# A recurrence step whose reset gate is formed ahead of the reciprocal, and inner norms scaled on VectorE

## The chip, the core and the metric

One core of a Trainium2 chip runs the whole program. The metric is the device time of one execution in microseconds (us). Engines are named as in the profile: PE is the matrix engine (PEld its weight loads), DVE the vector engine, ACT the scalar engine, POOL the GpSimd engine, SP the engine that issues most DMAs.

## What is computed

The input x is 4 batches of 512 tokens of width 128. Four layers follow one another, each added to x: a transformer block with self and context attention, a causal attention block with a dense mixture of 8 experts, a recurrent decoder, and an expert-choice mixture. The change is in the third layer and in the part of the second that runs beside it.

The recurrent layer takes 512 steps, one for each token, and each needs the state of the one before:

```
proj = h @ W
attn = softmax(enc_hiddens . proj)            # 77 context rows
context = attn @ enc_hiddens
gx = concat([x_t, context]) @ kernel + bias   # columns for z, r, candidate
gh = h @ recurrent_kernel
z = sigmoid(xz + hz);  r = sigmoid(xr + hr)
cand = tanh(xh + r * hh)
h = z * h + (1 - z) * cand
```

The layer in front of it, whose tail is computed beside the recurrence, has these norms; g and b are the norm's gain and bias, `layernorm` subtracts the mean and multiplies with the root of 1/(variance + eps):

```
h = layernorm(out, g, b)        # norm "g" of the names below, ahead of the experts
...experts weighted by a gate...
y = layernorm(moe, g, b)        # norm "h": added to x
x = layernorm(x + y)            # norm "i": the recurrence's input; norm "j" stands before the last layer
```

## The kernel before

Function `recurrence` runs both. Its "main" work is a Python loop over t in 0 to 511 that is unrolled on every engine. The order on each engine's queue is written out by hand; engines wait for one another through semaphores, and an instruction that waits holds back everything behind it on its engine.

The main chain of a step, by the lines of the profile: PE forms the scores from the state (L2068, L2074) and the state's own gate products (L2080). DVE takes the maximum of the scores (L2583) and copies the own products (L2589 or L2591, tile `own`). ACT makes the exponentials `p_t` (L2248), not yet divided by their sum. PE multiplies them with a table `gate_w` (helper `gate_products`, L1818): first the 32 columns for r together with two columns that give the sum of the exponentials (`ps_r`, `ps_total`, 34 columns), then the 64 columns for candidate and z (`ps_cz`). DVE takes the reciprocal of the sum (L2593, `rtotal`), then `pre_r` = r's product * rtotal + own (L2596), and `own` <- the other products * rtotal + own (L2599). ACT takes tanh of half of pre_r (L2251) and of half of pre_z (L2253). DVE forms the candidate's argument with a scan (L2603, `c_in`), ACT its tanh (L2255), DVE transposes (L2608, L2610) and forms the next state with another scan (L2614), on which PE's L2068 of the next step waits.

Beside this, each step carries pieces of "background" work, for the token tiles g = 1, 2, 3 (tile 0 is done before): attention in units (8 head pairs times 4 batches, a unit starting every 2 steps for g = 1 and 2, every 3 steps for g = 3), then the norm g and the gates, then 32 chunks of expert work, then the norms h and i, which give the recurrence the input of its next 128 steps. Three tables name the steps: attention of g starts at step 0, 110 and 219; the norm g at 71, 181 and 325; experts at 76, 186 and 330; the norms h and i (table `FIRST`) at 113 and 120, 223 and 231, 367 and 373. So the norms h and i of tile g fall into the attention of tile g + 1, and those of tile 3 into steps with little other work. Norm j stands at 383, 392 and 401. On PE background stands in `after_gates` (behind the gate products, ahead of the next L2068) and `ahead_of_gates` (ahead of the gate products). On ACT it stands in `after_exp` (ahead of L2251) and `after_candidate` (behind the step's last main operation), on DVE in `before_maximum` and `after_maximum`, both ahead of `own`. POOL runs `after_history`, at its own pace.

A norm takes these steps counted from its FIRST: 0 statistics (DVE, L2370), 1 moments (DVE, L2375), 2 `norm_scales` on POOL (L2271 to L2277: add eps, power -0.5, mean * rstd, times -1; 4 instructions), 3 `normalise` on ACT (L2111: two tiles in `after_exp`, two in `after_candidate`), 4 `turn_rows` on PE (L1931) and `take_rows` on ACT. For h there is no turn: POOL multiplies with the gain at step 4 (`gain_rows`, L2284) and adds to x at step 5 (`add_rows`, L2289). `BULK` names the steps behind norm i in which PE forms the input products for the next 128 tokens (L1985), one batch a step, four steps.

POOL also scales attention probabilities (`scale_probs`: a power, L2300, and a multiplication, L2304, which waits for the step's `c_in`) and forms the power for the query and key norms (L2296). PE turns the scaled probabilities (L1894).

## Time and profile before

| | us |
|---|---|
| median of 3 runs | 2823.57 |
| lowest and highest | 2823.46, 2825.21 |
| the profiled execution | 2822.87 |
| its span in the trace | 2821.0 |
| busy in the span: PE, DVE, ACT, POOL | 2447.3, 1887.3, 1567.0, 1002.9 |

The recurrence begins at 908 us (first L2583) and its last state is ready at 2707 us, so it takes 1799 us of the span, 3.51 us a step. A row of the timeline gives start, duration, engine, line, operation, what it writes and reads, and how often; in brackets stands the idle time of the engine before it and what ended it. The duration holds the time until the result is written; the next instruction of the same engine that waits for nothing may start before that.

### The profile page before, as it was taken

To read this page: it belongs to the slowest core of one execution; us is meant where nothing else is said; L and a number is where in the kernel's file an instruction comes from. 1 tells how busy PE (TensorE), PEld (TensorE's weight loads), DVE (VectorE), ACT (ScalarE), POOL (GpSimd) and SP (SyncE) were. 2 spreads that over 40 slices of the span, in tenths; PEclk is the share of its full clock that TensorE was granted. 3 is DMA by queue.
4 is the path that set the end of the run, shared out by engine and by line. 5 is a ranking of instruction groups with operands and counts; after the bars stand their busy time and mean duration, and the time that the engine had idled before them with its cause. 6 is when DMAs were issued, how large, how long until landed. Compare 5 with 4: busy or idle time off the path is not lost. (4 is left out here: it accounts for less than half of the span.)

```text
span 2821.0 us, 137474 instructions
## 1 busy us (share of the span) xinstructions
PE 2447.3 (87%) x57364; PEld 1663.9 (59%) x57364; DVE 1887.3 (67%) x7210; ACT 1567.0 (56%) x5258; POOL 1002.9 (36%) x2005
## 2 busy tenths in 40 slices
PE   6999999988988999798999897998879777666669
PEld 4666666666555555565555565666656545444449
DVE  4666666775553777677677677777767766776553
ACT  4777777643453666576666575666657443333322
POOL 2000000042110676466677465566636311001026
PEclk9999999999999999999999999999999999999989
DMA  4000000000012000011100010100001000000013
GB/s 155 5 5 5 5 8 5 2 12 5 14 37 72 24 19 15 11 43 31 27 17 15 14 44 23 27 11 14 8 7 43 6 20 7 6 7 7 6 49 88
DMA packets 51898, 64.80 MB, mean 23 GB/s; under 512 B 7432, under 2 KB 36560, under 8 KB 51152
## 3 DMA queue, kind: packets, MB, share of 16 engines
q1 hardware_dynamic: 47184, 50.32, 5.9%
q8 instruction: 456, 7.47, 1.1%
q0 software_dynamic: 4096, 5.67, 1.0%
q14 instruction: 162, 1.33, 0.2%
HBM read 46.38 MB, written 9.60 MB: 20 GB/s over the span
## 5 line engine op out<-in xcount | busy, mean ns | idle before, releaser
L2330 POOL TENSOR_TENSOR gru_terms<-gru_states,gru_signs 128x8 f32<-128x8 f32 x512 | 104.3, 204 | 687.6 <-DVE gru_states L2614 687.1
L2068 PE MATMUL gru_ps_sr<-score_w,gru_states 128*32 128x78 f32 x4096 | 175.1, 243 | 183.3 <-DVE gru_states L2614 173.7
L2248 ACT ACTIVATE gru_p_t<-gru_ps_tc,gru_negmax 128x12 f32<-128x12 f32 x512 | 138.9, 271 | 338.6 <-DVE gru_negmax L2583 322.0
L2251 ACT ACTIVATE gru_th_r<-gru_pre_r 128x32 f32<-128x32 f32 x512 | 119.2, 233 | 303.5 <-DVE gru_pre_r L2596 303.4
L2304 POOL TENSOR_SCALAR bg_probs<-bg_probs,bg_arsum 128x256 f32<-128x256 f32 (+2 forms) x192 | 240.9, 1255 | 86.4 <-DVE gru_c_in L2603 80.4
L1818 PE MATMUL gru_ps_tc<-ctx_gate_w,gru_p_t 128*4 128x64 f32 x12288 | 267.8, 219 | 2.0 <-issue 1.9
L1818 PE MATMUL gru_ps_sr<-ctx_gate_w,gru_p_t 128*4 128x34 f32 x12288 | 189.4, 194 | 78.7 <-ACT gru_p_t L2248 76.3
L2068 PEld LDWEIGHTS gru_ps_sr<-score_w,gru_states 128*32 128x32 f32 x4096 | 81.0, 107 | 292.2 <-DVE gru_states L2614 273.9
L313 ACT ACTIVATE self_probs<-self_sc,self_negmax 128x512 f32<-128x512 f32 x256 | 176.7, 698 | 112.1 <-DVE self_negmax L351 112.1
L1818 PEld LDWEIGHTS gru_ps_sr<-ctx_gate_w,gru_p_t 128*4 128x4 f32 x12288 | 120.1, 86 | 196.9 <-ACT gru_p_t L2248 179.9
L351 DVE TENSOR_REDUCE self_negmax<-self_sc 128x1 f32<-128x512 f32 x256 | 158.9, 683 | 109.4 <-PE self_sc L236 109.4
L2080 PE MATMUL gru_ps_ox<-late,gru_states 128*4 128x128 f32 x4096 | 225.2, 272 | 0.0
L2583 DVE TENSOR_REDUCE gru_negmax<-gru_ps_sr 128x1 f32<-128x77 f32 x512 | 119.8, 234 | 128.6 <-PE gru_ps_sr L2068 120.8
L2593 DVE RECIPROCAL gru_rtotal<-gru_ps_sr 128x1 f32<-128x1 f32 x512 | 85.9, 168 | 163.4 <-PE gru_ps_sr L1818 159.8
L2603 DVE TENSOR_TENSOR_SCAN gru_c_in<-gru_th_r,gru_own 128x64 f32<-128x64 f32 x512 | 149.2, 291 | 60.8 <-ACT gru_th_r L2251 6.7
L1818 PEld LDWEIGHTS gru_ps_tc<-ctx_gate_w,gru_p_t 128*4 128x4 f32 x12288 | 185.4, 86 | 2.3 <-issue 2.0
L193 POOL TENSOR_SCALAR self_n_var<-self_n_mv 128x4 f32<-128x4 f32 x4 | 0.9, 232 | 504.6 <-DVE self_n_mv L379 504.6
L2610 DVE STREAM_TRANSPOSE gru_terms<-gru_cand 128x32 f32<-128x32 f32 x512 | 113.9, 222 | 94.4 <-ACT gru_cand L2255 94.4
L2074 PE MATMUL gru_ps_tc<-gru_states,score_w 128*32 128x1 f32 (+1 forms) x12288 | 170.1, 167 | 0.0
L2255 ACT ACTIVATE gru_cand<-gru_c_in 128x32 f32<-128x32 f32 x512 | 118.3, 231 | 86.0 <-DVE gru_c_in L2603 86.0
L2074 PEld LDWEIGHTS gru_ps_tc<-gru_states,score_w 128*32 128x32 f32 (+1 forms) x12288 | 155.2, 106 | 0.0
L2589 DVE TENSOR_TENSOR gru_own<-gru_ps_ox,late 128x128 f32<-128x128 f32 x480 | 135.9, 283 | 19.7 <-PE gru_ps_ox L2080 15.5
(433 smaller groups left out, 6510.0 us busy)
## 6 DMA issues: line engine op xcount, KB each, us to landing
bg_w<-in_moe_w SPq DMA_DIRECT2D x48, 256.0 KB, 3.2
bg_wa<-in_wqkv SPq DMA_DIRECT2D x24, 192.0 KB, 2.4
moe_w<-in_moe_w SPq DMA_DIRECT2D x16, 256.0 KB, 2.9
best_w_sb<-in_ec_w SPq DMA_DIRECT2D x16, 256.0 KB
x_products<-late SPq DMA_DIRECT2D x16, 240.0 KB, 2.4
late<-x_products SPq DMA_DIRECT2D x240, 16.0 KB
pair_w<-in_wqkv SPq DMA_DIRECT2D x16, 192.0 KB, 2.4
cross_scratch<-ctab_raw SPq DMA_DIRECT2D x16, 154.0 KB
```

The source lines that it names most:

```text
L313: act.activation(probs[:, u, :], sc[u % 4][:], ACT.Exp, bias=negmax[:, u:u + 1], accum_out=total[:, u:u + 1]).then_inc(s_exp, 1)
L351: dve.tensor_reduce(negmax[:, u:u + 1], sc[u % 4][:], axis=AX.X, op=ALU.max, negate=True).then_inc(s_max, 1)
L1818: last = pe.matmul(bank[32 * c:32 * c + B, 0:hi - lo], p_t[:, B * k:B * k + B], gate_w[:, k, GATE_ALL * c + lo:GATE_ALL * c + hi], start=k ...
L2068: last = pe.matmul(ps_s[32 * b:32 * b + 32, :], state(t)[:, b:b + 1].broadcast_to([P, 32]), score_w[:, b, 0:CTX + 1], start=True, stop=Tru ...
L2074: last = pe.matmul(ps_t[32 * b:32 * b + keys, B * k + b:B * k + b + 1], score_w[:, b, 32 * k:32 * k + keys], state(t)[:, b:b + 1], start=T ...
L2080: last = pe.matmul(ps_own[32 * c:32 * c + B, :], state(t), h_w[:, c, :], start=from_rows(t), stop=True, tile_position=(0, 32 * c), skip_gr ...
L2248: act.activation(p_t[:], ps_t, ACT.Exp, bias=negmax[:, 0:1]).then_inc(s_exp, 1)
L2251: act.activation(th_r[:, 1:64:2], pre_r[:], ACT.Tanh, scale=0.5).then_inc(s_thr, 1)
L2304: pool.tensor_scalar(row, row, arsum[:, j:j + 1], None, ALU.mult).then_inc(s_apn, 1)
L2583: dve.tensor_reduce(negmax[:], ps_s[:, 0:CTX], axis=AX.X, op=ALU.max, negate=True).then_inc(s_max, 1)
L2589: dve.tensor_tensor(own[:, 0:256:2], ps_own, x_in[:, k % 2, t % CHUNK, :], ALU.add).then_inc(s_own, 1)
L2603: dve.tensor_tensor_scan(c_in[:], th_r[:], own[:, 192:256], 0.0, ALU.mult, ALU.add).then_inc(s_cin, 1)
```

## The change

1. The table `gate_w` gets 2.0 instead of 1.0 in its second extra column, so that the gate products give the sum of the exponentials and its double. One DVE copy for each of three tables becomes two instructions.
2. In the step, DVE first forms `pre_r` = own * sum + r's product, straight from PSUM (the sum is the pointer scalar of the fused operation), and then the reciprocals of the sum and of its double. ACT's tanh for r gets the second reciprocal as its scale, and waits for it. All else of the step reads `rtotal` as before.
3. The norms' scaling leaves ACT. For g, i and j DVE subtracts the mean and multiplies with rstd in one operation a tile. For h DVE forms (y - mean) * gain and then x + that * rstd, 4 + 4 fused operations; POOL's `gain_rows` and `add_rows` go. POOL's `norm_scales` keeps 2 of its 4 instructions.
4. Steps: a new function `after_own` on DVE stands between `own` and `pre_r`. Norm g and j: two tiles in `after_maximum`, two in `after_own`, step 3. Norm h: two tiles each in `after_own` at steps 2 and 3 (gain) and 4 and 5 (add). Norm i: two each in `after_own` at steps 3 and 4. FIRST of h becomes 114, 224, 367 and of i 120, 230, 373. The turn of i stands at step 126, 235 and 378 (before 124, 235, 377), and BULK one step behind it (127, 236, 379; before 125, 236, 378).

```diff
-                dve.tensor_copy(by_chunk[:, :, 32:GATE_C], key.rearrange("p (a b) -> p a b", a=1).broadcast_to([P, 4, 2]))
+                every_chunk = key.rearrange("p (a b) -> p a b", a=1).broadcast_to([P, 4, 1])
+                dve.tensor_copy(by_chunk[:, :, 32:33], every_chunk)
+                dve.tensor_scalar(by_chunk[:, :, 33:GATE_C], every_chunk, 2.0, None, ALU.mult)
...
-        FIRST = {n: {"g": GATING[n[0]], "h": EXPERTS[n[0]] + C + 5, "i": EXPERTS[n[0]] + C + {1: 12, 2: 13, 3: 11}[n[0]]}[n[1]] for n in NORMS}
+        FIRST = {n: {"g": GATING[n[0]], "h": EXPERTS[n[0]] + C + (5 if n[0] == 3 else 6), "i": EXPERTS[n[0]] + C + (11 if n[0] == 3 else 12)}[n[1]] for n in NORMS}
...
-        BULK = {0: 0, **{g: FIRST[g, "i"] + 5 for g in (1, 2, 3)}}
+        TURN_I = {g: FIRST[g, "i"] + (6 if g == 1 else 5) for g in (1, 2, 3)}
+        BULK = {0: 0, **{g: TURN_I[g] + 1 for g in (1, 2, 3)}}
...
-            def normalise(at, norm, j):
-                act.wait_ge(s_rstd, 4 * at + 4)
-                act.activation(normed(norm)[:, j, :], source(norm)[:, j, :], ACT.Identity, bias=nshift[:, j:j + 1],
-                               scale=rstd[:, j:j + 1]).then_inc(s_norm, 1)
...
+                act.wait_ge(s_rt, t + 1)
                 act.wait_ge(s_prer, t + 1)
-                act.activation(th_r[:, 1:64:2], pre_r[:], ACT.Tanh, scale=0.5).then_inc(s_thr, 1)
+                act.activation(th_r[:, 1:64:2], pre_r[:], ACT.Tanh, scale=rtotal[:, 1:2]).then_inc(s_thr, 1)
...
-                pool.tensor_tensor(nshift[:], mv[:, :, 0], rstd[:], ALU.mult).then_inc(s_rstd, 1)
-                pool.tensor_scalar(nshift[:], nshift[:], -1.0, None, ALU.mult).then_inc(s_rstd, 1)
...
-            def gain_rows(at, norm):
-            def add_rows(at, norm):
...
+            def normalise(at, norm, j):
+                dve.wait_ge(s_rstd, 2 * at + 2)
+                dve.tensor_scalar(normed(norm)[:, j, :], source(norm)[:, j, :], mv[:, j, 0:1], rstd[:, j:j + 1], ALU.subtract, ALU.mult)\
+                   .then_inc(s_norm, 1)
+            def centre(at, norm, j):
+                dve.wait_ge(s_aggr, B * at + j + 1)
+                dve.scalar_tensor_tensor(out=xn[:, j, :], in0=source(norm)[:, j, :], scalar=mv[:, j, 0:1], in1=g_rows[:, j, :],
+                                         op0=ALU.subtract, op1=ALU.mult).then_inc(s_gain, 1)
+            def add_normed(at, norm, j):
+                dve.wait_ge(s_rstd, 2 * at + 2)
+                dve.wait_ge(s_gain, (norm[0] - 1) * B + j + 1)
+                dve.wait_ge(s_shift, norm[0])
+                dve.scalar_tensor_tensor(out=own_tiles(x, norm[0])[:, j, :], in0=xn[:, j, :], scalar=rstd[:, j:j + 1],
+                                         in1=own_tiles(x, norm[0])[:, j, :], op0=ALU.mult, op1=ALU.add).then_inc(s_norm, 1)
...
                     dve.tensor_copy(own[:, 0:256:2], ps_own).then_inc(s_own, 1)
+                after_own(t)
                 dve.wait_ge(s_rmm, t + 1)
-                dve.reciprocal(rtotal[:], ps_total).then_inc(s_rt, 1)
+                dve.wait_ge(s_own, t + 1)
+                dve.scalar_tensor_tensor(out=pre_r[:], in0=own[:, 0:64:2], scalar=ps_total, in1=ps_r[:, 0:32],
+                                         op0=ALU.mult, op1=ALU.add).then_inc(s_prer, 1)
+                dve.reciprocal(rtotal[:], ps_r[:, 32:GATE_C]).then_inc(s_rt, 1)
                 dve.wait_ge(s_rt, t + 1)
-                dve.wait_ge(s_own, t + 1)
-                dve.scalar_tensor_tensor(out=pre_r[:], in0=ps_r[:, 0:32], scalar=rtotal[:, 0:1], in1=own[:, 0:64:2],
-                                         op0=ALU.mult, op1=ALU.add).then_inc(s_prer, 1)
```

## Rows read from the trace of the kernel before

**Rows 1.** The page's first line.
```profile
span 2821.0 us, 137474 instructions
```

**Rows 2.** Timeline of one late step, DVE and ACT: start, us, engine, line, operation.
```profile
2662.55 0.17 DVE L2593 RECIPROCAL gru_rtotal<-gru_ps_sr 128x1 f32<-128x1 f32 x1 [0.36 <-PE gru_ps_sr L1818]
2662.76 0.25 DVE L2596 SCALAR_TENSOR_TENSOR gru_pre_r<-gru_ps_sr,gru_rtotal,gru_own 128x32 f32<-128x32 f32 x1
2662.93 0.28 DVE L2599 SCALAR_TENSOR_TENSOR gru_own<-gru_ps_tc,gru_rtotal,gru_own 128x64 f32<-128x64 f32 x1
2663.04 0.23 ACT L2251 ACTIVATE gru_th_r<-gru_pre_r 128x32 f32<-128x32 f32 x1 [0.99 <-DVE gru_pre_r L2596]
2663.23 0.23 ACT L2253 ACTIVATE gru_th_z<-gru_own 128x32 f32<-128x32 f32 x1
2663.31 0.29 DVE L2603 TENSOR_TENSOR_SCAN gru_c_in<-gru_th_r,gru_own 128x64 f32<-128x64 f32 x1
...
2664.15 0.18 DVE L2614 TENSOR_TENSOR_SCAN gru_states<-gru_factors,gru_terms 128x12 f32<-128x12 f32 x1
```

**Rows 3.** Who waited for L2614 in the whole trace (us, times).
```profile
  PEld gru_ps_sr L2068: 273.9, 354
```

**Rows 4.** Waits (us, times, longest) of stretches 909:1135, 1187:1298, 1783:2092, 2226:2710, in order.
```profile
PEld gru_ps_sr L2068 <- DVE gru_states L2614: 14.2, 57, 0.7
...
PEld gru_ps_sr L2068 <- DVE gru_states L2614: 2.4, 4, 0.8
...
PEld gru_ps_sr L2068 <- DVE gru_states L2614: 45.7, 84, 1.6
...
PEld gru_ps_sr L2068 <- DVE gru_states L2614: 149.5, 143, 1.1
```

**Rows 5.** Windows: length, busy PE, PEld, DVE, ACT, POOL (count); PE clock, DMA, GB/s.
```profile
1758.30:1763.00 4.70, 4.31 (x98) 2.92 (x100) 2.86 (x12) 3.28 (x13) 2.75 (x5) 0.64 0.02 5
...
1376.00:1544.00 168.00, 160.40 (x4685) 100.17 (x4677) 126.44 (x517) 115.45 (x471) 121.94 (x225) 1.00 0.06 16
```

**Rows 6.** Timeline: POOL in step 123, PEld in the attention of tile 2.
```profile
1343.38 1.04 POOL L2273 TENSOR_TENSOR bg_rstd<-bg_var,bg_power 128x4 f32<-128x4 f32 x1
...
1444.38 0.31 PEld L1894 LDWEIGHTS gru_bg_turn<-early,bg_probs 128*128 128x128 f32 x3 [0.39 <-POOL bg_probs L2304]
```

**Rows 7.** Timeline, ACT's norm operations that waited, in four steps.
```profile
1316.96 0.88 ACT L2111 ACTIVATE bg_xn<-y,bg_shift,bg_rstd 128x128 f32<-128x128 f32 x2 [0.95 <-POOL bg_shift L2277]
...
1345.07 0.88 ACT L2111 ACTIVATE bg_xn<-x,bg_shift,bg_rstd 128x128 f32<-128x128 f32 x2 [0.65 <-POOL bg_shift L2277]
...
1726.64 0.88 ACT L2111 ACTIVATE bg_xn<-y,bg_shift,bg_rstd 128x128 f32<-128x128 f32 x2 [1.08 <-POOL bg_shift L2277]
...
1756.41 0.88 ACT L2111 ACTIVATE bg_xn<-x,bg_shift,bg_rstd 128x128 f32<-128x128 f32 x2 [1.24 <-POOL bg_shift L2277]
```

**Rows 8.** Timeline, state scans ending steps 115, 116, 233 and 235, step 234's reciprocal.
```profile
1313.64 0.19 DVE L2614 TENSOR_TENSOR_SCAN gru_states<-gru_factors,gru_terms 128x12 f32<-128x12 f32 x1
1318.84 0.24 DVE L2614 TENSOR_TENSOR_SCAN gru_states<-gru_factors,gru_terms 128x12 f32<-128x12 f32 x1
...
1753.14 0.33 DVE L2614 TENSOR_TENSOR_SCAN gru_states<-gru_factors,gru_terms 128x12 f32<-128x12 f32 x1
...
1755.09 0.17 DVE L2593 RECIPROCAL gru_rtotal<-gru_ps_sr 128x1 f32<-128x1 f32 x1 [0.46 <-PE gru_ps_sr L1818]
...
1762.85 0.18 DVE L2614 TENSOR_TENSOR_SCAN gru_states<-gru_factors,gru_terms 128x12 f32<-128x12 f32 x1
```

**Rows 9.** Timeline ahead of the recurrence, the same norm operations on DVE.
```profile
896.85 1.14 DVE L1277 SCALAR_TENSOR_TENSOR moe_xn<-y,moe_mv,late 128x128 f32<-128x128 f32 x4
...
901.14 1.11 DVE L1222 TENSOR_SCALAR moe_xn<-x,moe_mv,moe_rstd 128x128 f32<-128x128 f32 x4 [0.60 <-ACT moe_rstd L1188]
```

**Rows 10.** The two scans' durations in ns: min/median/max, first and last start.
```profile
L2603 DVE TENSOR_TENSOR_SCAN gru_c_in<-gru_th_r,gru_own x512: 290/291/294, 910.7 to 2706.2; 128x64 f32<-128x64 f32 x171
...
L2614 DVE TENSOR_TENSOR_SCAN gru_states<-gru_factors,gru_terms x512: 181/182/636, 911.5 to 2707.1; 128x12 f32<-128x12 f32 x171
```

More of the change, by code:

```diff
@@ L1567, in recurrence @@
         p_t = sb("p_t", 3 * B)
-        negmax, rtotal = sb("negmax", 1), sb("rtotal", 1)
+        negmax, rtotal = sb("negmax", 1), sb("rtotal", 2)
         own = sb("own", 5 * 64)
@@ L1604, in recurrence @@
         xn = tile("xn", B, P)
-        stats, mv, var, rstd, nshift, power = (tile(n, *k) for n, k in (
-            ("stats", (B, 6)), ("mv", (B, 2)), ("var", (B,)), ("rstd", (B,)), ("shift", (B,)), ("power", (B,))))
+        stats, mv, var, rstd, power = (tile(n, *k) for n, k in (
+            ("stats", (B, 6)), ("mv", (B, 2)), ("var", (B,)), ("rstd", (B,)), ("power", (B,))))
         logits, shifted, expd, gate = (tile(n, B, E) for n in ("logits", "shifted", "expd", "gate"))
@@ L1620, in recurrence @@
         gates_t = ctx.enter_context(nc.sbuf_tensor("bg_gates_t", [E, B * P], F32))
-        s_stat, s_aggr, s_rstd, s_norm, s_gain, s_shift, s_x, s_turn, s_cols, s_xt = (
-            late_sem(n) for n in ("stat", "aggr", "rstd", "norm", "gain", "shift", "x", "turn", "cols", "xt"))
+        s_stat, s_aggr, s_rstd, s_norm, s_gain, s_shift, s_turn, s_cols, s_xt = (
+            late_sem(n) for n in ("stat", "aggr", "rstd", "norm", "gain", "shift", "turn", "cols", "xt"))
         s_lg, s_gstep, s_gexp, s_gate, s_gt, s_gte, s_b2, s_y = (
@@ L1745, in norms_at, with turns_at @@
                     yield at, norm
+        def turns_at(t):
+            return [n for n in norms_at(t, 4) if n[1][1] in "gj"] + [(at, n) for at, n in enumerate(NORMS) if n[1] == "i" and t == TURN_I[n[0]]]
         def gating_at(t, first):
@@ L2011, in after_gates @@
                     busy = True
-                for at, norm in norms_at(t, 4):
-                    if norm[1] != "h":
-                        turn_rows(at, norm)
+                for at, norm in turns_at(t):
+                    turn_rows(at, norm)
                 for g, n, m in units_at(t, "project"):
@@ L2198, in after_exp @@
                         take_out(g, n, m)
-                for at, norm in norms_at(t, 3):
-                    normalise(at, norm, 0)
-                    normalise(at, norm, 1)
                 for at, g in gating_at(t, 7):
@@ L2230, in after_candidate @@
                         take_out(g, n, m)
-                for at, norm in norms_at(t, 3):
-                    normalise(at, norm, 2)
-                    normalise(at, norm, 3)
-                for at, norm in norms_at(t, 4):
-                    if norm[1] != "h":
-                        take_rows(at, norm)
+                for at, norm in turns_at(t):
+                    take_rows(at, norm)
                 for at, g in gating_at(t, 10):
@@ L2306, in after_history @@
             def after_history(t):
-                for at, norm in norms_at(t, 4):
-                    if norm[1] == "h":
-                        gain_rows(at, norm)
-                for at, norm in norms_at(t, 5):
-                    if norm[1] == "h":
-                        add_rows(at, norm)
                 for at, g in gating_at(t, 5):
@@ L2545, in after_maximum @@
                         do(at, g)
+                for at, norm in norms_at(t, 3):
+                    if norm[1] in "gj":
+                        normalise(at, norm, 0)
+                        normalise(at, norm, 1)
                 for g in history_at(t, 1):
@@ L2556, in after_maximum, with after_own @@
                     reverse_eights(t - REVERSE)
+            def after_own(t):
+                for at, norm in norms_at(t, 3):
+                    if norm[1] in "gj":
+                        normalise(at, norm, 2)
+                        normalise(at, norm, 3)
+                for j in (0, 2):
+                    for at, norm in norms_at(t, 2 + j // 2):
+                        if norm[1] == "h":
+                            centre(at, norm, j)
+                            centre(at, norm, j + 1)
+                    for at, norm in norms_at(t, 4 + j // 2):
+                        if norm[1] == "h":
+                            add_normed(at, norm, j)
+                            add_normed(at, norm, j + 1)
+                    for at, norm in norms_at(t, 3 + j // 2):
+                        if norm[1] == "i":
+                            normalise(at, norm, j)
+                            normalise(at, norm, j + 1)
             dve.memset(power[:], -0.5).then_inc(s_init, 1)
```

13 lines of the change are left out of this document (3 added, 10 removed).

## Prediction, made before the changed kernel ran

> **What bounds the kernel now.** I read the page first: the span is 2821.0 us [rows 1], and 1799 of it are the recurrence. Then the timeline of one late step, to get the order inside a step [rows 2]; then the waits of the whole trace and of stretches of it, to see in which steps the order of DVE and ACT sets the length [rows 3, 4]; then windows and single rows where a step is longer than its neighbours [rows 5 to 8].
>
> In the late step, count from the start R of the reciprocal (2662.55): pre_r starts at +0.21, `own` (its candidate and z part, L2599, "cz" below) at +0.38, tanh for r at +0.49, tanh for z at +0.68, c_in at +0.76, the next state's scan at +1.60 [rows 2]. The state then releases PE's L2068. That wait occurs 354 times, 273.9 us in all [rows 3], so about 158 of the 512 steps do not wait for the state at all: there PE is still at background work. By stretch: 57 of the 354 lie in the attention of tile 1 and are short (14.2 us, 0.25 each), 4 in the first experts, 84 in the attention of tile 3 (45.7 us), 143 in the tail (149.5 us) [rows 4]; the 70 that are left are in the gates, the other experts and the steps between stages. In the attention of tile 2 there is none: PE is busy 160.40 of 168 us at full clock [rows 5], and its weight loads follow POOL's multiplication [rows 6].
>
> **The recurrence's tail.** Removed: pre_r's wait for the reciprocal. New order: pre_r at R, since it needs only the products; its sum is a pointer scalar. The reciprocal is behind it with no wait for it. L2599 started 0.17 after L2596, which lasts 0.25, with no wait between them [rows 2]; I take 0.17 for this pair. The reciprocal lasts 0.17 [rows 2], so both reciprocals are ready at R + 0.34. ACT's tanh starts 0.03 after the end of what it waits for (2663.01 to 2663.04 [rows 2]): R + 0.37, not R + 0.49, 0.12 earlier. But cz still reads `rtotal`: before it started at +0.38, 0.21 after the reciprocal had started and 0.17 behind pre_r; now it starts 0.17 + 0.21 = 0.38 at most, or 0.37. It is not earlier, or by 0.01. c_in needs both: tanh's end, 0.37 + 0.23 = 0.60, and 0.04 more (3.27 to 3.31 [rows 2]) = 0.64; and cz's end, 0.37 + 0.28 = 0.65, and the same 0.03 to 0.04 = 0.68 to 0.69. So **cz is late next**: c_in moves from +0.76 to +0.69, the state from +1.60 to +1.53. The gain is 0.07 a step, not 0.12.
>
> What no row shows: this fused form with its scalar and a tensor in PSUM and in0 in SBUF. From below: no start distance under 0.17 stands in rows 2; 0.02, the rounding of two starts, would give 0.09 a step. From above: the distance grows to 0.21, the largest between two such operations in rows 2, and 0.04 of the 0.07 goes. I take 0.17, the row of the same 32 elements. Two elements for one in the reciprocal, and a pointer for the constant in tanh's scale: from 0 to 0.01 (32 columns last 0.25 and 64 0.28 [rows 2], so 1 column more is under 0.01); taken 0. ACT's added wait on the reciprocal has nothing behind it that is not already behind the wait for pre_r (tanh z, then c_in's tanh); z's tanh is released by cz at +0.65 and starts at +0.68 as before.
>
> **Which steps pass it on.** Those in which PE's L2068 waits for the state, by more than 0.07. Attention of tile 1: 57 waits of 0.25 mean [rows 4]. About every second step has one, some 0.17 of each is there even where PE has just got free, and what sets the length of these steps is POOL's chain, which hangs on the step's start and not on c_in: 0. Attention of tile 2 and most expert steps: no wait for the state: 0. The remaining 354 - 57 = 297 pass it on: 297 * 0.07 = **20.8 us** (tail 143, or 10.0; attention of tile 3 84, or 5.9; the others 70, or 4.9). With 0.09: 26.7; with 0.03: 8.9.
>
> **The norms.** Removed from ACT: 4 operations of 0.44 (two 0.88 [rows 7]) a norm, half of them ahead of tanh r, and their wait for POOL's rstd. That wait cost 0.95, 0.65, 1.08 and 1.24 us in four steps [rows 7]. Three of them fall in steps 116, 226 and 234, which are 1.55 to 1.6 longer than their neighbours; step 116 is 5.20 us (1313.64 to 1318.84), and 234 is the first half of the 9.71 us from 1753.14 to 1762.85 [rows 8]. Afterwards DVE's operation needs rstd too, but h's first operation (centre) does not, h's second is two steps behind POOL's power, and i's waits at step 3 as before. So those three stalls go: 4.75 us. In step 123 the wait (0.65 before) goes over to DVE, ahead of pre_r, where everything of the step is queued behind it. POOL's rstd is written at 1343.38 + 1.04 = 1344.42 [rows 6]; two operations on DVE (0.50, below), then pre_r at 1344.95 and c_in 0.69 later, 1345.64. Before, ACT's two operations ran from 1345.07 to 1345.95 [rows 7] and tanh r, 0.25 to c_in, stood behind them: about 1346.1. So 0.4 are gained. Steps behind the stalls (118, 124, 125, 229, 235) are long too: PE's granted clock falls, to a mean of 0.64 from 1758.3 to 1763 [rows 5], right behind the stall in which PE waited for the state, and step 235 takes 9.71 - 5.15 = 4.56. Without the stalls I expect full clock there. Against a neighbour of 3.6, step 235 is worth 1.0; for all five I count 3.05, an estimate with 0 and 5 as ends. In sum 8.2.
>
> Added: DVE's operations last as those of tile 0 do, four in 1.14 and four in 1.11 [rows 9], 0.25 to 0.28 each from start to start; two in `after_own` take 0.50. What hides them in the loaded steps of h and i is DVE's wait for the gate products ahead of the reciprocal, 0.46 in step 234 [rows 8]: 0.50 is 0.04 too long, in 18 steps: 0.7. Norms g and j have two tiles ahead of `own` and two behind it, 1.0 in one step, six times, in light steps whose cover is 0.36 [rows 2] and DVE's pause ahead of `own`, 0.3: pre_r is later by 0.30: 1.8. The tables' three extra instructions, before the recurrence: each no longer than the 0.17 of a small operation [rows 2], 0.5 if all is on the path and 0 if none: inside the rounding. Bulk and turn are moved, not added; POOL loses 4 instructions in h and 2 in each other norm and no queue gets longer. Net of the norms: 8.2 - 0.7 - 1.8 = **5.7 us**, between 0 (nothing gained behind the stalls, twice the additions) and 8.
>
> **Trap weighed.** A DVE operation with two SBUF inputs beside a wide POOL operation is seen to stretch: L2614, 0.18 in the middle, goes to 0.636, while L2603 goes from 290 only to 294 [rows 10]; the 0.33 at 1753.14 is such a row [rows 8]. Centre and add_normed have two SBUF tensors, but POOL's wide scaling of probabilities waits for c_in and so runs later than `after_own`; what can meet them is POOL's power, 1.04 [rows 6]. The Trainium skill's page "SBUF — State Buffer", section "Who interferes with whom", says that a Vector instruction with two SBUF inputs contends with a GpSimd one that reads SBUF and that whoever comes second waits for the whole of the other; the trace agrees as to L2614 (0.636 against 0.181).
>
> **Sum.** 20.8 + 5.7 = 26.5. The profiled execution is 2822.87 (span 2821.0 and 1.9 around it), 0.7 below the median of 2823.57. 2822.87 - 26.5 = 2796.4, as a median 2797.0.
>
> **The rivals.**
> 1. *The reciprocal is held until pre_r is finished* (slower). Then it starts at R + 0.28, is ready at 0.45, tanh r starts at 0.48, cz at 0.49 and c_in at 0.49 + 0.28 + 0.035 = 0.805: 0.045 later than before, 297 * 0.045 = 13.4 lost, 5.7 kept: 2831. It decides from a distance of 0.24 between the two starts (0.17 + 0.07), and the whole time passes the old one at 0.26. For it: the scalar in PSUM is new. Against it: L2599, which also reads PSUM with a pointer scalar, was not held [rows 2]. The page "VectorE: DVE Perf Modes" of the Trainium skill, section "Two Vector instructions with no wait between them", has an instruction held until all earlier ones are finished where operands start in different quadrants; all of these start at partition 0, so by it nothing is held, and the trace agrees (0.17 behind an operation of 0.25). Chance 0.08.
> 2. *The gain vanishes in the attention of tile 3*: its 84 waits are 0.54 mean [rows 4], but if POOL's chain through its probabilities comes last at PE in the next step, 5.9 is absorbed: 2803. The same time comes out if the norms are worth nothing (2803), with stalls turned into DVE's waits. Together 0.17.
> 3. *POOL beside DVE's new operations*: 1.04 lost in up to 6 loaded steps, about 5: 2802. Chance 0.07.
> 4. *All steps gain*: a step bound by PE hands on 0.07 too, since `after_gates` begins with the gate products and all of DVE's and ACT's later work comes earlier; 207 steps more, 14.5: 2782. Against it: PE is 95% busy there [rows 5]. Chance 0.05.
> 5. *The change doesn't do what it says*: tanh r keeps waiting for something else, as z's or POOL's order. In rows 2 nothing but pre_r is in front of it. Chance 0.01, about 2817.
>
> **How the numbers follow.** The forecast, 0.62: 2797. Only case 1 is slower. The range takes in cases 2 and 3 and the start distance between 0.17 and 0.20 (up to 12 less gained: 2809) with the norms' lower bound beside it, 2813; below it takes 0.09 a step (5.9 more) and the norms at 8 (2.3 more) and rounding, 2786. Cases 1 and 4 are out, with a little of the forecast's own. Faster by over 0.2% (about 5.6 us, what a measurement can tell from no change) 0.86; within it 0.06, from distances near 0.23; slower 0.08.
>
> **What would show it.** Right: pre_r at R, reciprocal at +0.17, tanh r at +0.37, c_in at +0.69, state at +1.53; tail steps 3.23 instead of 3.30; attention of tile 2 and experts unchanged; no stall at steps 116, 226, 234 and neighbours under 4 us; at step 123 DVE waits for POOL; steps of g and j longer by 0.3. Wrong: the reciprocal at +0.25 or later; c_in released by tanh r; the tail unchanged, with DVE's time before R grown; norms' stalls back on DVE ahead of pre_r.

## The result, and the profile after

| | before | changed |
|---|---|---|
| median, us | 2823.46 (5 runs) | 2837.97 (5 runs) |
| lowest and highest | 2822.61, 2825.21 | 2834.30, 2838.83 |
| span of the profiled execution | 2821.0 | 2832.5 |

The changed kernel is slower: ratio 1.0047, interval 1.0035 to 1.0058. The forecast was 2797. The medians stand 14.5 us apart. The two profiled executions, which the traces below come from, stand 11.5 apart: the one of the changed kernel (2834.30) was the fastest of its five.

A late step, beside the one in [rows 2], timeline of DVE and ACT in the changed kernel (start, us, engine, line, operation):

```profile
2676.60 0.25 DVE L2611 SCALAR_TENSOR_TENSOR gru_pre_r<-gru_own,gru_ps_sr 128x32 f32<-128x32 f32 x1 [0.37 <-PE gru_ps_sr L1825]
2676.77 0.16 DVE L2613 RECIPROCAL gru_rtotal<-gru_ps_sr 128x2 f32<-128x2 f32 x1
2676.96 0.32 ACT L2246 ACTIVATE gru_th_r<-gru_pre_r,gru_rtotal 128x32 f32<-128x32 f32 x1 [0.86 <-DVE gru_rtotal L2613]
2676.99 0.28 DVE L2616 SCALAR_TENSOR_TENSOR gru_own<-gru_ps_tc,gru_rtotal,gru_own 128x64 f32<-128x64 f32 x1
2677.31 0.23 ACT L2248 ACTIVATE gru_th_z<-gru_own 128x32 f32<-128x32 f32 x1
2677.38 0.29 DVE L2620 TENSOR_TENSOR_SCAN gru_c_in<-gru_th_r,gru_own 128x64 f32<-128x64 f32 x1
...
2678.22 0.18 DVE L2631 TENSOR_TENSOR_SCAN gru_states<-gru_factors,gru_terms 128x12 f32<-128x12 f32 x1
```

Counted from R, the start of the first operation (2676.60): reciprocals +0.17, tanh r +0.36, cz (L2616, L2599 before) +0.39, c_in +0.78, state +1.62. Before, c_in stood at +0.76 and the state at +1.60. So the new order did put tanh r 0.12 earlier, and c_in came 0.02 later (0.03 in the median of 65 late steps: 0.755 and 0.783). Two things differ from the forecast of +0.69: tanh r lasts 0.32 instead of 0.23, and c_in starts 0.11 behind the end of cz (2677.27), not 0.04.

The next table has the time from the first state to the last, from the scans' starts in each profile, by stage. The ramp ahead of the first state is left out, since it differs by up to 4.8 us between profiles (the first state stood from 911.5 to 916.3), and by 3.9 between two kernels of the experiments whose code up to the recurrence is the same (912.0 and 915.9):

| steps | before | changed | difference |
|---|---|---|---|
| attention of tile 1 (1-65) | 227.4 | 226.0 | -1.3 |
| gates, experts (66-112) | 164.4 | 167.0 | +2.6 |
| norms h, i of tile 1 (113-127) | 63.1 | 59.3 | -3.8 |
| attention of tile 2 (128-174) | 177.8 | 180.0 | +2.1 |
| gates, experts (175-222) | 168.6 | 170.1 | +1.5 |
| norms h, i of tile 2 (223-240) | 70.2 | 68.5 | -1.7 |
| attention of tile 3 (241-333) | 323.1 | 326.4 | +3.4 |
| gates, experts (334-366) | 118.1 | 117.8 | -0.3 |
| tail (367-511) | 482.9 | 490.8 | +7.9 |
| all | 1795.5 | 1805.9 | +10.3 |

Most of the loss is in small pieces: 230 steps are each 0.02 to 0.04 longer, 7.2 us together. The gains are where the norms stand. The wait of PE for the state in attention of tile 3 and in the tail, changed kernel, beside [rows 4]:

```profile
PEld gru_ps_sr L2074 <- DVE gru_states L2631: 48.4, 84, 1.4
...
PEld gru_ps_sr L2074 <- DVE gru_states L2631: 156.0, 142, 1.6
```

About as many waits as before (84 and 143), and longer in the mean: 0.58 for 0.54 in attention of tile 3, 1.10 for 1.05 in the tail.

The norms' operations moved as described. Step 116, from the scans at its ends, beside [rows 8]:

```profile
1316.42 0.18 DVE L2631 TENSOR_TENSOR_SCAN gru_states<-gru_factors,gru_terms 128x12 f32<-128x12 f32 x1
...
1320.25 0.23 DVE L2631 TENSOR_TENSOR_SCAN gru_states<-gru_factors,gru_terms 128x12 f32<-128x12 f32 x1
```

The step takes 3.83 us instead of 5.20: the stall is gone. But the products for the next 128 tokens, which moved two steps later (from steps 125 to 128 to steps 127 to 130), now stand in step 130 too, where none stood before (3.81 us). The scan that begins it, the product, the scan that ends it:

```profile
1374.08 0.18 DVE L2631 TENSOR_TENSOR_SCAN gru_states<-gru_factors,gru_terms 128x12 f32<-128x12 f32 x1
...
1377.21 1.02 PE L1992 MATMUL gru_ps_ox<-late,x_t 128*120 128x384 f32 x2
...
1378.66 0.23 DVE L2631 TENSOR_TENSOR_SCAN gru_states<-gru_factors,gru_terms 128x12 f32<-128x12 f32 x1
```

This step takes 4.58 us. Step 74, a step of norm g, timeline of DVE:

```profile
1166.58 0.18 DVE L2631 TENSOR_TENSOR_SCAN gru_states<-gru_factors,gru_terms 128x12 f32<-128x12 f32 x1
...
1167.38 0.59 DVE L2355 TENSOR_SCALAR bg_xn<-y,bg_mv,bg_rstd 128x128 f32<-128x128 f32 x2
...
1168.09 0.59 DVE L2355 TENSOR_SCALAR bg_xn<-y,bg_mv,bg_rstd 128x128 f32<-128x128 f32 x2
1168.60 0.24 DVE L2611 SCALAR_TENSOR_TENSOR gru_pre_r<-gru_own,gru_ps_sr 128x32 f32<-128x32 f32 x1
```

Counted from the first scan, pre_r stands at 2.02, in a step in which it otherwise stands at 1.71. Each of six steps is longer by this 0.31.

### The profile page after: what moved, and what is told of

It reads as the page before. It is cut to its first block and busy times, and to the rows that moved or that the text cites. A ratio compares the mean times of both kernels' runs of the same rounds, so it can differ in the third digit from the quotient of the medians.

```text
span 2832.5 us, 138492 instructions
## 1 busy us (share of the span) xinstructions
PE 2449.0 (86%) x57364; PEld 1664.8 (59%) x57364; DVE 1903.3 (67%) x7273; ACT 1615.1 (57%) x5210; POOL 993.0 (35%) x1975
## 5 line engine op out<-in xcount | busy, mean ns | idle before, releaser
L2246 ACT ACTIVATE gru_th_r<-gru_pre_r,gru_rtotal 128x32 f32<-128x32 f32 x512 | 165.5, 323 | 255.5 <-DVE gru_rtotal L2613 248.4
L2611 DVE SCALAR_TENSOR_TENSOR gru_pre_r<-gru_own,gru_ps_sr 128x32 f32<-128x32 f32 x512 | 129.1, 252 | 156.6 <-PE gru_ps_sr L1825 150.9
L2599 DVE TENSOR_REDUCE gru_negmax<-gru_ps_sr 128x1 f32<-128x77 f32 x512 | 119.9, 234 | 125.6 <-PE gru_ps_sr L2074 118.2
L2616 DVE SCALAR_TENSOR_TENSOR gru_own<-gru_ps_tc,gru_rtotal,gru_own 128x64 f32<-128x64 f32 x512 | 145.8, 285 | 37.0 <-PE gru_ps_tc L1825 3.3
```

The costliest lines, as they stand in the source:

```text
L2246: act.activation(th_r[:, 1:64:2], pre_r[:], ACT.Tanh, scale=rtotal[:, 1:2]).then_inc(s_thr, 1)
L2611: dve.scalar_tensor_tensor(out=pre_r[:], in0=own[:, 0:64:2], scalar=ps_total, in1=ps_r[:, 0:32], op0=ALU.mult, op1=ALU.add).then_inc(s_pre ...
L2616: dve.scalar_tensor_tensor(out=c_and_z, in0=ps_cz, scalar=rtotal[:, 0:1], in1=own[:, 64:192:2], op0=ALU.mult, op1=ALU.add).then_inc(s_prec ...
```

## The experiments

**The two halves.** First each half of the change alone. The edit of the one is the diff's table, `rtotal` and recurrence hunks on the kernel before; that of the other is everything else.

> The kernel before with the recurrence's edits alone (table of 1 and 2, pre_r ahead of the reciprocals, tanh r with the reciprocal as its scale); the norms stay on ACT. Theory A (ACT's tanh with a pointer for its scale lasts 0.32 instead of 0.23 us, and eats what the new order gives): c_in at R+0.78 instead of +0.76, a tail step of 3.33 instead of 3.30, 0.025 in some 300 steps = 7.5, and 1.0 in step 0: 2832. Theory B (the loss comes from the norms' operations that moved to DVE): this kernel is faster than before, 2803 to 2820.

Measured 2842.11, ratio 1.0066 (1.0050 to 1.0083). C_in at R+0.78, state at +1.63. First to last state 1813.1 us, 17.6 more than before. Theory A has the direction and the place of c_in right, but the loss is twice what it expects. Of the 17.6 us, 7.3 are in 235 steps that are each 0.02 to 0.04 longer, as A has it. Another 2.95 are in the one step 408 (8.57 for 5.62), in which the granted clock of TensorE was 0.50, the lower of its two levels (1.2 GHz), throughout; it had fallen 1.2 us ahead of the step, after 2.2 us in which PE was busy for 1.63. Before the change, the clock was 1.00 until some 2 us into this step, all of them busy, and 0.70 in the step's mean. The other 7.4 us are spread over the rest of the steps, and why is open.

> The changed kernel with the recurrence's order of before: the norms' edits and steps alone. Theory A: the stalls on POOL in steps 116, 226 and 234 go, six steps of the norms g and j are 0.3 longer: 3 to 7 us faster than before, 2816 to 2820. Theory B: slower than before, 2826 to 2838.

Measured 2824.57 against 2824.66, ratio 0.9999 (0.9989 to 1.0009). B is refuted: the norms lose nothing. A's 3 to 7 us of gain aren't in the times either. In the profile the recurrence is 1791.2 us, 4.3 less than before, but the profiled execution was the fastest of ten, 4.6 under their median. Step 234 in it, DVE:

```profile
1752.27 0.34 DVE L2628 TENSOR_TENSOR_SCAN gru_states<-gru_factors,gru_terms 128x12 f32<-128x12 f32 x1
...
1755.83 0.34 DVE L2628 TENSOR_TENSOR_SCAN gru_states<-gru_factors,gru_terms 128x12 f32<-128x12 f32 x1
```

The step takes 3.56 us; before it took 5.15.

**The pointer.** Two kernels take the price of tanh's pointer apart from the rest. A pointer here is a scale that the operation reads from a tile, one value for each partition, instead of a constant.

```
-                act.activation(th_r[:, 1:64:2], pre_r[:], ACT.Tanh, scale=rtotal[:, 1:2]).then_inc(s_thr, 1)
+                act.activation(th_r[:, 1:64:2], pre_r[:], ACT.Tanh, scale=0.5).then_inc(s_thr, 1)
```

> The changed kernel, with the constant 0.5 as tanh r's scale instead of the second reciprocal, and the same waits: it leaves out the division of r's argument by the sum. Theory A (the pointer costs 0.09): tanh r lasts 0.23, c_in at R+0.69, state at R+1.53, tail steps 3.23, about 0.09 * 300 = 27 under the changed kernel: 2811. Rival C (what costs is the second wait, or the value that DVE has only just written): tanh r stays at 0.32 or starts later, 2830 to 2838.

Measured 2838.15, as the changed kernel. Timeline, DVE and ACT:

```profile
2622.45 0.25 DVE L2611 SCALAR_TENSOR_TENSOR gru_pre_r<-gru_own,gru_ps_sr 128x32 f32<-128x32 f32 x1 [0.36 <-PE gru_ps_sr L1825]
...
2622.82 0.23 ACT L2246 ACTIVATE gru_th_r<-gru_pre_r 128x32 f32<-128x32 f32 x1 [0.86 <-DVE gru_rtotal L2613]
2622.85 0.28 DVE L2616 SCALAR_TENSOR_TENSOR gru_own<-gru_ps_tc,gru_rtotal,gru_own 128x64 f32<-128x64 f32 x1
2623.17 0.23 ACT L2248 ACTIVATE gru_th_z<-gru_own 128x32 f32<-128x32 f32 x1
2623.24 0.29 DVE L2620 TENSOR_TENSOR_SCAN gru_c_in<-gru_th_r,gru_own 128x64 f32<-128x64 f32 x1
```

Tanh r lasts 0.23 again, and is over at 2623.05, but c_in waits until 2623.24: 0.19 behind it, and 0.11 behind the end of cz (2623.13). ACT's tanh z, which waits for the same cz, started at 2623.17, 0.04 behind it. Theory A as the whole cause falls: the price of the pointer is real, and in this kernel it is hidden behind something else. C's time (2830 to 2838) came out, but not what it said of tanh r, which neither lasted 0.32 nor started later. That a second wait costs something comes back below, at another instruction.

```
-                act.activation(th_r[:, 1:64:2], pre_r[:], ACT.Tanh, scale=0.5).then_inc(s_thr, 1)
+                act.activation(th_r[:, 1:64:2], pre_r[:], ACT.Tanh, scale=half[:, 0:1]).then_inc(s_thr, 1)
...
+            dve.memset(half[:], 0.5).then_inc(s_init, 1)
```

> The kernel before, with tanh r's scale 0.5 read from a tile that is filled once before the recurrence; nothing else. Theory A: tanh r lasts 0.32 instead of 0.23; its end (R+0.81) was last at c_in, so all of the 0.09 is in c_in in some 300 steps: +27, 2850. Rival C: no change, 2823.

Measured 2862.06, ratio 1.0143 (1.0126 to 1.0160): 37.4 us. Timeline, from the reciprocal on:

```profile
2601.49 0.17 DVE L2594 RECIPROCAL gru_rtotal<-gru_ps_sr 128x1 f32<-128x1 f32 x1 [0.36 <-PE gru_ps_sr L1818]
...
2601.98 0.33 ACT L2251 ACTIVATE gru_th_r<-gru_pre_r,gru_half 128x32 f32<-128x32 f32 x1 [0.99 <-DVE gru_pre_r L2597]
...
2602.34 0.29 DVE L2604 TENSOR_TENSOR_SCAN gru_c_in<-gru_th_r,gru_own 128x64 f32<-128x64 f32 x1 [0.20 <-ACT gru_th_r L2251]
```

The value was written long before, and tanh r is 0.09 longer all the same (0.324 for 0.233 in the median), so the price does not come from a value that has only just been written. C_in is at R+0.85, 0.09 later, 0.03 behind tanh r's end. By stage, 13.2 of the loss lies in the tail (0.09 in nearly each of 145 steps), 6.8 in the attention of tile 3, and 6.7 in the attention of tile 1, where most second steps are 0.26 longer. In the attention of tile 2 it is 1.5, in the three times 32 expert steps 2.5. Where the 0.26 comes from is shown below, at the kernel before with exchanged waits.

**The order of the waits.** What is special in c_in's 0.11? It has two waits, in this order: tanh r, then cz. In the kernel before, tanh r (+0.72) ended later than cz (+0.65), and c_in started 0.04 behind it; tanh r's wait is written first. Now cz, whose wait is written second, starts c_in. The next three kernels exchange the two lines.

```
-                dve.wait_ge(s_thr, t + 1)
                 dve.wait_ge(s_precz, t + 1)
+                dve.wait_ge(s_thr, t + 1)
                 dve.tensor_tensor_scan(c_in[:], th_r[:], own[:, 192:256], 0.0, ALU.mult, ALU.add).then_inc(s_cin, 1)
```

> The changed kernel with one pair of DVE's waits in the other order: ahead of c_in it waits first for L2616's result and then for tanh r. Theory D1 (the scan starts 0.39 behind L2616, though that lasts 0.28, since a wait for DVE's own result that stands directly at the instruction is seen late): c_in at R+0.72, tail steps 3.27, 0.06 in 300 steps, 2820. Theory D2 (0.39 is what the pair costs, whatever the waits): no change, c_in R+0.78, 2838.

Measured 2842.71, ratio 1.0064 (1.0048 to 1.0081); c_in at R+0.79, 0.01 later. D1's gain is refuted. D2 has c_in nearly right; the time is 5 above its 2838.

> The kernel before with the same two waits in the other order. In it tanh r's end (R+0.72) and L2599's start plus 0.38 (R+0.76) give the same time for c_in within 0.01. Theories D1 and D2: no change, c_in at R+0.76, 2824; below that only if the scan starts less than 0.03 behind tanh r.

Measured 2851.64, ratio 1.0097 (1.0080 to 1.0113): 26.2 us for two exchanged lines. Both theories missed it. Timeline:

```profile
2622.80 0.17 DVE L2593 RECIPROCAL gru_rtotal<-gru_ps_sr 128x1 f32<-128x1 f32 x1 [0.36 <-PE gru_ps_sr L1818]
...
2623.29 0.23 ACT L2251 ACTIVATE gru_th_r<-gru_pre_r 128x32 f32<-128x32 f32 x1 [0.99 <-DVE gru_pre_r L2596]
...
2623.62 0.29 DVE L2603 TENSOR_TENSOR_SCAN gru_c_in<-gru_th_r,gru_own 128x64 f32<-128x64 f32 x1 [0.18 <-ACT gru_th_r L2251]
```

Tanh r ends at 2623.52 as before (R+0.72), and c_in starts 0.10 behind it instead of 0.04.

These 0.07 are not all of the 26.2 us. In the attention of tile 1 most second steps are 0.26 longer, as in the kernel with the pointer. There the state's scan meets POOL's scaling of the probabilities. Before the change, and with the waits exchanged:

```profile
1015.79 0.94 POOL L2304 TENSOR_SCALAR bg_probs<-bg_probs,bg_arsum 128x256 f32<-128x256 f32 x1
1015.82 0.18 DVE L2614 TENSOR_TENSOR_SCAN gru_states<-gru_factors,gru_terms 128x12 f32<-128x12 f32 x1
```

```profile
1020.19 0.94 POOL L2304 TENSOR_SCALAR bg_probs<-bg_probs,bg_arsum 128x256 f32<-128x256 f32 x1
1020.30 0.39 DVE L2614 TENSOR_TENSOR_SCAN gru_states<-gru_factors,gru_terms 128x12 f32<-128x12 f32 x1
```

In the kernel before, the scan starts 0.03 behind POOL's operation in these steps and keeps its 0.18; with the waits exchanged it starts 0.11 behind it and lasts 0.39. In the 65 steps one scan was over 0.3 long before, and 27 are now: 5.4 of the 7.0 us lost there (in the kernel with the pointer also 27, 5.0 of 6.7).

> The changed kernel with the constant 0.5 as tanh r's scale (it leaves out the division of r's argument by the sum) and the two waits in the other order. Tanh r is over at R+0.60. Theory D1: c_in at R+0.71, 2815 to 2820. Theory D2: c_in at R+0.78 as with the constant alone, 2838.

Measured 2818.28, ratio 0.9972 (0.9963 to 0.9982), 20 us under the same kernel with the waits in the old order:

```profile
2624.61 0.25 DVE L2611 SCALAR_TENSOR_TENSOR gru_pre_r<-gru_own,gru_ps_sr 128x32 f32<-128x32 f32 x1 [0.39 <-PE gru_ps_sr L1825]
...
2624.98 0.23 ACT L2246 ACTIVATE gru_th_r<-gru_pre_r 128x32 f32<-128x32 f32 x1 [0.87 <-DVE gru_rtotal L2613]
2625.01 0.28 DVE L2616 SCALAR_TENSOR_TENSOR gru_own<-gru_ps_tc,gru_rtotal,gru_own 128x64 f32<-128x64 f32 x1
2625.33 0.23 ACT L2248 ACTIVATE gru_th_z<-gru_own 128x32 f32<-128x32 f32 x1
2625.33 0.29 DVE L2620 TENSOR_TENSOR_SCAN gru_c_in<-gru_th_r,gru_own 128x64 f32<-128x64 f32 x1
```

C_in now starts together with tanh z, 0.04 behind cz, at R+0.72. All these fit one rule, theory E: an instruction with two waits starts no sooner than 0.04 behind what its first-written wait is for, and no sooner than 0.10 behind what its second-written wait is for. It doesn't matter whether DVE itself or ACT gives the signal, so D1 was half right, and D2 falls.

**The reciprocal first.** The last of this group has the two reciprocals ahead of pre_r:

```
                 dve.wait_ge(s_rmm, t + 1)
+                dve.reciprocal(rtotal[:], ps_r[:, 32:GATE_C]).then_inc(s_rt, 1)
                 dve.wait_ge(s_own, t + 1)
                 dve.scalar_tensor_tensor(out=pre_r[:], in0=own[:, 0:64:2], scalar=ps_total, in1=ps_r[:, 0:32],
                                          op0=ALU.mult, op1=ALU.add).then_inc(s_prer, 1)
-                dve.reciprocal(rtotal[:], ps_r[:, 32:GATE_C]).then_inc(s_rt, 1)
```

> The changed kernel with the two reciprocals ahead of pre_r, and no wait between them (pre_r still multiplies own with the sum). Theory D (what is last at c_in in the changed kernel is DVE's own pair: L2616, which waits for the reciprocals, and the scan of c_in 0.39 behind its start): the reciprocals start at R instead of R+0.17, pre_r some 0.15 later; L2616 has both behind it at R+0.32 instead of +0.39, so c_in is 0.02 to 0.07 earlier unless tanh r (start R+0.45, end +0.77) is last, c_in R+0.76 to +0.80: the same as the changed kernel or up to 6 us less, 2832 to 2838. Theory A (the pointer in tanh r is what costs): c_in follows tanh r, R+0.735 if pre_r starts at +0.10: 2825.

Measured 2833.85, ratio 1.0032 (1.0020 to 1.0045):

```profile
2622.87 0.17 DVE L2610 RECIPROCAL gru_rtotal<-gru_ps_sr 128x2 f32<-128x2 f32 x1 [0.36 <-PE gru_ps_sr L1825]
2622.95 0.23 DVE L2612 SCALAR_TENSOR_TENSOR gru_pre_r<-gru_own,gru_ps_sr 128x32 f32<-128x32 f32 x1
2623.26 0.28 DVE L2616 SCALAR_TENSOR_TENSOR gru_own<-gru_ps_tc,gru_rtotal,gru_own 128x64 f32<-128x64 f32 x1
2623.28 0.32 ACT L2246 ACTIVATE gru_th_r<-gru_pre_r,gru_rtotal 128x32 f32<-128x32 f32 x1 [0.91 <-DVE gru_pre_r L2612]
...
2623.65 0.29 DVE L2620 TENSOR_TENSOR_SCAN gru_c_in<-gru_th_r,gru_own 128x64 f32<-128x64 f32 x1
```

The time lies in theory D's range, and c_in (+0.78) follows cz as D has it; A, with 2825, falls again. Pre_r starts 0.08 behind the reciprocal, sooner than I had thought (0.15), and is over at R+0.31. Yet tanh r starts 0.10 behind that, at +0.41: it waits for the reciprocals first and for pre_r second. And cz, whose DVE inputs are ready, starts only at +0.39: it waits for the reciprocals first and for PE's products second. This is E at two more places, on ACT too and with PE's signal.

**Where the two prices come from.** The traces of all these kernels have a record of the sequencers that decides this. The second-written wait of each pair is an instruction of its own, `EVENT_SEMAPHORE`, ahead of the operation, in all 512 steps. The first-written wait has no record of its own. ACT's second-written wait ahead of tanh r (line 2245) and DVE's ahead of c_in (line 2619), in the changed kernel:

```profile
L2245 ACTq EVENT_SEMAPHORE  x512: 17/17/17, 910.1 to 2717.2; - x171
...
L2619 DVEq EVENT_SEMAPHORE  x512: 21/21/21, 910.9 to 2717.6; - x171
```

Line 2244, the first-written of the pair for tanh r, and line 2618, that for c_in, have no instruction. In late steps the extra instruction starts 0.03 to 0.04 behind the signal that it waits for, in every one of the 13 kernels, and the operation 0.06 to 0.07 behind the extra instruction wherever that one was last: together the 0.10. A wait without an instruction of its own costs the 0.04 alone, first-written or single (tanh z, 0.04 behind cz). In the kernel before it was in fact a tie: the extra instruction for cz stood at +0.69 and c_in 0.07 behind it.

**The forecast of theory E.** Reciprocals first, and in each pair the later wait written first:

```
+                act.wait_ge(s_prer, t + 1)
                 act.wait_ge(s_rt, t + 1)
-                act.wait_ge(s_prer, t + 1)
...
+                dve.wait_ge(s_czmm, t + 1)
                 dve.wait_ge(s_rt, t + 1)
-                dve.wait_ge(s_czmm, t + 1)
```

> The changed kernel with the reciprocals ahead of pre_r, and in each pair of waits the one that comes last written first: tanh r waits for pre_r and then for the reciprocals, L2616 for its products and then for the reciprocals; c_in keeps tanh r first. Theory E (a DVE or ACT instruction with two waits starts 0.04 behind what its first wait is for, but 0.10 behind what its second is for; the seven kernels up to here fit it): pre_r +0.08 to +0.31, tanh r +0.35 to +0.67, L2616 +0.33 to +0.61, c_in at +0.71, state +1.55, tail steps 3.25: 0.05 under the kernel before in some 300 steps, 15 us, with the norms at 0: 2809. Rival F (the orders of waits did something else, and the first kernels fit by chance): c_in stays at +0.76 to +0.80, 2824 to 2838.

Measured 2814.21, ratio 0.9964 (0.9951 to 0.9978):

```profile
2604.32 0.17 DVE L2610 RECIPROCAL gru_rtotal<-gru_ps_sr 128x2 f32<-128x2 f32 x1 [0.36 <-PE gru_ps_sr L1825]
2604.40 0.23 DVE L2612 SCALAR_TENSOR_TENSOR gru_pre_r<-gru_own,gru_ps_sr 128x32 f32<-128x32 f32 x1
2604.64 0.28 DVE L2616 SCALAR_TENSOR_TENSOR gru_own<-gru_ps_tc,gru_rtotal,gru_own 128x64 f32<-128x64 f32 x1
2604.67 0.32 ACT L2246 ACTIVATE gru_th_r<-gru_pre_r,gru_rtotal 128x32 f32<-128x32 f32 x1 [0.85 <-DVE gru_pre_r L2612]
...
2605.03 0.29 DVE L2620 TENSOR_TENSOR_SCAN gru_c_in<-gru_th_r,gru_own 128x64 f32<-128x64 f32 x1
...
2605.88 0.18 DVE L2631 TENSOR_TENSOR_SCAN gru_states<-gru_factors,gru_terms 128x12 f32<-128x12 f32 x1
```

Tanh r +0.35, cz +0.32, c_in +0.71, state +1.56: the forecast within 0.01 at each. F is refuted. The recurrence takes 1781.4 us, 14.1 less than before, where 15 were expected. The median is 9.8 under the kernel before and 5 above the forecast of 2809. In the profiled executions the difference is the ramp ahead of the recurrence, which was 4.8 longer here. Over the 13 profiles the ramp scatters by as much, and the kernel before has the shortest.

> The kernel before with the recurrence of the ordered kernel, the norms on ACT as before. Theory E: c_in at R+0.71 as well; with norms that are worth nothing (2824.57 for the norms alone against 2824.66) 2809, with norms worth the 4 us of the one profile 2813. Rival F: 2824 to 2842.

Measured 2816.31, ratio 0.9970 (0.9958 to 0.9982). That is above both forecasts (2809, and 2813 with norms worth 4 us), as the ordered kernel was above its own. C_in stands at R+0.71, as expected. The norms are worth 2.1 us in the medians, which the scatter of the runs doesn't tell from nothing, and 3.2 in the profiles (1784.6 against 1781.4).

> The ordered kernel with the scaling of the norms g and j back on ACT (and their two POOL operations), h and i on DVE. The six steps 74, 184, 328, 386, 395 and 404 were each 0.31 longer with the new norms; if that is the operations' time ahead of pre_r, 1.8 us come back: 2807 by theory E. If ACT's operations ahead of tanh r cost as much, no change: 2809.

Measured 2811.98, ratio 0.9962 (0.9947 to 0.9976), 2.2 under the ordered kernel in the median; its interval and that of the ordered kernel overlap, and its recurrence, 1782.5, isn't shorter. The trace settles it all the same: the six steps came back from 3.57 to 3.27 each, 1.8 us together, as expected. Step 408 took them away again, with 7.67 for 6.04 us at a mean granted clock of 0.56 for 0.72. It is the fastest median of the case, 12.0 under the kernel before.

The kernels' late steps, as medians of some 60 steps each, counted from R; in brackets the place, as written, of the wait for what started c_in; in the kernel before and in the ordered one both would start it at the same time:

| kernel | tanh r ends | cz ends | c_in | state |
|---|---|---|---|---|
| before | 0.72 (first) | 0.65 (second) | 0.76 | 1.60 |
| before, swapped | 0.72 (second) | 0.65 | 0.82 | 1.67 |
| before, pointer | 0.81 (first) | 0.65 | 0.85 | 1.69 |
| changed | 0.69 | 0.68 (second) | 0.78 | 1.63 |
| changed, swapped | 0.69 (second) | 0.68 | 0.79 | 1.63 |
| changed, constant | 0.60 | 0.68 (second) | 0.78 | 1.63 |
| changed, constant, swapped | 0.60 | 0.68 (first) | 0.71 | 1.56 |
| reciprocal first | 0.74 | 0.68 (second) | 0.78 | 1.63 |
| ordered | 0.68 (first) | 0.61 (second) | 0.71 | 1.56 |

## Why the prediction was wrong

**The step that failed: c_in's wait for cz.** The prediction put c_in 0.03 to 0.04 behind cz's end, at +0.69; it starts 0.10 behind it, at +0.78, later than before the change (+0.76). So the gain of 0.07 in 297 steps (20.8 us) became a loss. Much of the frame held: pre_r at R, reciprocals at +0.17, tanh r at +0.37, "cz is late next". Rival 1 did not happen: the reciprocal started 0.17 behind pre_r, which lasts 0.25, though the scalar comes from PSUM, and pre_r kept its 0.25. Two terms of the tail's sum were wrong:

- *"cz's end, 0.37 + 0.28 = 0.65, and the same 0.03 to 0.04".* It is 0.10 to 0.11, since cz is c_in's second-written wait, which is an instruction of its own. [rows 2] could not tell: there cz's end plus 0.10 (0.76) and tanh r's end plus 0.04 (0.76) are the same number. I took the delay of one wait for the other and didn't ask what the row bounds: it only said that cz costs no more than 0.10. Cz itself was at +0.39, not +0.37, because PE's products are its second-written wait now; before, it had one wait. From there the sum comes out: cz's end at 0.68 and 0.10 more is +0.78.
- *"A pointer for the constant in tanh's scale: from 0 to 0.01".* It is 0.09 (0.32 against 0.23). In the changed kernel it cost nothing, since tanh r (+0.69) ended ahead of what c_in really waited for. Here I looked at the number of columns alone, and groups of the trace of before had the price. The groups by shape, ACT, three operations of 128 columns, with no pointer, with one (scale) and with two (bias and scale); the third also reads SBUF where the first two read PSUM:

```profile
L2177 ACT ACTIVATE bg_o<-gru_bg_out 128x128 f32<-128x128 f32 x96 | 26.6, 277 | 1.7 <-PE gru_bg_out L1908 0.9
...
L2157 ACT ACTIVATE bg_k_own<-gru_bg_out,late 128x128 f32<-128x128 f32 x32 | 11.8, 368 | 7.1 <-PE gru_bg_out L1868 7.0
...
L2111 ACT ACTIVATE bg_xn<-x,bg_shift,bg_rstd 128x128 f32<-128x128 f32 x12 | 5.2, 483 | 1.9 <-POOL bg_shift L2277 1.9
```

277, 368, 483 ns: 0.09 for the first pointer, and 0.115 for the second and the other memory together. The Trainium skill, page "ScalarE: Activation LUTs", section "What ACT_TABLE_LOAD costs", says that each `[128,1]` pointer operand adds about 93 ns to an ACTIVATE; the trace agrees, with 323 against 233 in tanh r.

The wait alone took the gain: with the pointer gone c_in stayed at +0.78 and the time at 2838. The pointer alone would not have: tanh r's end at 0.69 and 0.04 more is +0.73, an estimate from these rows, and still 0.03 earlier than before. No kernel has just this. Exchanging the waits is not the same, since it puts tanh r behind the second-written wait (0.69 and 0.10, +0.79); with the pointer gone as well, c_in came at +0.71.

**Which steps pass it on: near for gains, short for losses.** Between the two kernels with the constant, 0.07 a step made the recurrence 18.7 us shorter, of which 1.5 are step 408 with its clock: the rest is some 250 steps' worth; I had 297. Losses spread further: 37.4 / 0.09 = 415 and 26.2 / 0.07 = 374 steps' worth. The attention of tile 1, which I had put at 0, lost 6.7 and 7.0 us, for there a later scan is caught beside POOL and lasts 0.2 longer. The prediction's trap had the collision, and looked for it only at the norms' new operations. It also had the later of the two wait for the whole of the other: here the scan was over 0.44 ahead of POOL's end (1020.69 and 1021.13).

**Step 0.** A term that I didn't have. ACT loads a table ahead of its first tanh; before, that ran from 909.03 on, while pre_r was being made. Now it starts 0.08 behind the signal of the second-written wait, whose instruction stands ahead of it: in the changed kernel at 910.20, behind pre_r's end at 910.12; with the reciprocals' wait written second, 0.08 behind theirs. Step 0 takes 2.83 from R to its state instead of 1.87: 1.0 us once. The load in the kernel before and in the changed one:

```profile
909.03 1.28 ACT L2251 ACT_TABLE_LOAD   x1
```

```profile
910.20 1.28 ACT L2246 ACT_TABLE_LOAD   x1 [0.97 <-DVE gru_pre_r L2611]
```

**The norms: right in the trace, small in the time.** 5.7 were expected. The profiles give 4.3 (norms alone), 7.2 (1813.1 against 1805.9) and 3.2 (ordered). Of the 7.2, 3.0 are step 408 (8.57 against 5.55), whose length goes with the granted clock (0.50 against 0.72) and not with the norms: it took 7.74 with the new norms in the kernel with the constant, and 5.90 with the old ones in the ordered kernel. So 3.2 to 4.3 is what the traces agree on. The medians give 0.1, 4.1 (from two groups of runs, in which the kernel before stood 1.2 apart) and 2.1. The stalls of 116 and 234 went (1.37 and 1.56), that of 226 too with the norms alone, step 235 went from 4.56 to 3.54, step 123 gained 0.37 where 0.4 was expected, and g and j cost 0.31 in six steps. That the fall of the clock in step 235 comes from the stall ahead of it isn't shown: the kernel before with exchanged waits kept the stall (5.21), and had full clock and 3.70 in step 235. Not as put: step 118 stayed at 4.77 for 4.73, which I had counted as gained, and the moved products were not free, since the steps they left gave back more than expected (step 125 from 5.84 to 3.67) and steps 130 and 131 lost 0.77 and 0.75. Rival 3 did not happen: DVE's new operations last 337 to 344 ns in the mean of every group, beside POOL's power or not.

**The rivals.** None had the right cause. The slower one was given 0.08 with 2831; it needed a held reciprocal. A rival "c_in's wait for cz is longer than tanh r's" was missing. In the sum the recurrence's edits cost 17 to 18 us and the norms' gave back about 4, neither free of what the clock did in step 408. Two slips of the sum changed nothing: rival 4's 207 steps should be 215 (512 - 297), and "up to 12 less gained" belongs to a distance of 0.21, while 0.20 gives 9 (297 * 0.03).

## What to carry to other kernels

When an operand of a chain arrives earlier, only the next one's arrival is left, and its distance to the consumer has to be known by itself: where a row shows two inputs ready at the same moment, it bounds each delay and measures neither. Price an operation in the form it will have, pointer operands and number of waits included, from a group of the same form. Where an instruction waits for two things, write first the wait that is satisfied last, and check that order again whenever a change alters which one that is. And ask of a small delay what it will meet: here the state's scan had some 0.04 us to spare beside POOL.
